# Attention block on one Trainium2 core: the low halves of the probabilities split by columns between VectorE and GpSimd

## Chip, cores, metric

One core of a Trainium2 chip. The metric is the device time of one execution in microseconds (us), the median of several runs. Lower is better.

## What is computed

For each of 16 images of 1024 tokens and 512 channels (all float32):

```
xn  = silu(group_norm(x, 32 groups) * scale + offset)
q, k, v = split(xn @ w_qkv)            # 8 heads of 64
P   = softmax(q k^T / 8)               # per head, 1024 x 1024
out = (P v) @ w_out + b_out + x
```

To keep float32-like accuracy with float16 matmuls, values are held as two float16 parts: a high part (the value rounded) and a low part (what the rounding lost). The probabilities have a high part `Ph` and a low part `Pl = P32 - Ph`, and both are multiplied with v.

## The kernel before

An image's attention is cut into 64 **units**. Unit v works on head v // 8, on one half (512) of the query tokens, and on two blocks of 128 keys; its exponentials are a tile of 128 rows by 1024 columns, in which columns 0 to 511 belong to the first key block (i = 0) and 512 to 1023 to the second (i = 1). The image has 4 steps of 16 units; `Fori` runs over images. Every engine walks through the same list of iterations (s, u), with v = 16 s + u, in an order written out by hand, and they meet only at semaphores. I number iterations by v within the image.

In iteration v, **TensorE** (L1009 to L1023) does: the scores of unit v into the PSUM tile `ST[v % 2]` (L970, L971), once exp_done tells that unit v - 2 has been read; the score maxima of a later unit into `TP` (L905), once VectorE has drained `TP`; the product of the probabilities of unit v - 2 with v (`times_v`, L976 to L1007, the matmuls at L1004); then a **side** job where the table `SIDE` (L79) has one. These are projections to q and k ("qk"), to v ("v") or to the output ("out"), each 12 matmuls of 512 columns (L891), and short transposes of the attention output ("ot", L941) or of the input ("xt", L947). In iterations 2, 6, 10, ... a "shift" (L912) comes last.

**ScalarE** in iteration v rounds the side result of iteration v - 1 to its high part (for example L521, L537), then writes the exponentials of unit v twice: `P32[v % 2]` in float32 (L559) and `Ph[v % 4]` in float16 (L562), which raises exp_done. `P32` has two buffers, so L559 of unit v waits until the low part of unit v - 2 has been made.

**VectorE** in iteration v (L777 to L803) copies the shift of v - 1 (L711), makes the low part of the side result of v - 1 (L650, L655, L662, or L667 for "out"), takes the maxima out of `TP` (L707, and every fourth time the small L699), and **in odd iterations only** makes the whole low part of unit v - 1 (`low_probs`, L755, L760). After that, in every fourth iteration, it adds up the sums of four units (L767, L768). At v = 7 it also moves half of v (L775, `move_v`). In iterations 28 to 31 it takes statistics of the next image's input (L721), in 38 it makes the coefficients of the group norm (L735 to L745), and from 40 to 47 eight pieces of the silu (L750, L753).

**GpSimd** in iteration v (L474 to L488) makes, **in even iterations only**, the whole low part of unit v - 1 (L460). In iterations 1, 5, 9, ... it normalises (L467), which waits for VectorE's sums of that same iteration. In iteration 37 it runs the Newton steps (L434 to L441), from 40 to 47 the low part of the silu pieces (L447), and now and then it adds the bias (L452).

So low parts of even units come from VectorE, which counts them in lo_dve, and those of odd units from GpSimd, which counts them in lo_pool. TensorE waits for one of the two before unit v's products (L981 to L984), ScalarE before L559 (L555 to L558). **SyncE** issues the DMAs, in order: the input (L330), the residual (L336), the output (L342), and after the last "qk" of a step six copies of q and k (`place`, L353).

Of the kernel before, what the change touches and what calls it, by code (L numbers as in the profile page):

```python
# [10 lines left out]
ALU = mybir.AluOpType  # L11
# [3 lines left out]
B, TOK, CH = 16, 1024, 512  # L15
# [5 lines left out]
HALF = 512  # L21
# [3 lines left out]
UNITS = 64  # L25
# [155 lines left out]
def wait(eng, sem, count):  # L181

    if not isinstance(count, int) or count > 0:
        eng.wait_ge(sem, count)


def conv_attention(nc, x, gamma, beta, w_qkv, w_out, b_out, out):
# [4 lines left out]
    with ctx:  # L192
# [109 lines left out]
        lo_dve = sem("lo_dve")  # L302
# [107 lines left out]
        def _(pool):  # L410
# [44 lines left out]
            def low_probs(b, v):  # L455

                pool.wait_ge(exp_done, UNITS * b + v + 1)

                wait(pool, pv_done, UNITS * b + v - 3)
                nc.gpsimd.tensor_tensor(Pl[:, v % 4, :], P32[:, v % 2, :], Ph[:, v % 4, :], ALU.subtract  # L460
                                        ).then_inc(lo_pool, 1)

            def normalise(b, half):
# [10 lines left out]
            def step(b, s, first=False, last=False):  # L474
                for u in range(16):
                    v = 16 * s + u
                    if v % 2 == 0 and not (first and v == 0):
                        low_probs(b, v - 1)
                    if v % 4 == 1 and not (first and v == 1):
                        normalise(b, v // 4 - 1)  # L480
                    if s == 2 and u == 5 and not last:
                        newton(b + 1)
                    if s == 2 and 8 <= u and not last:
                        low_xn(b + 1, u - 8)
                    if s == 3 and u < 4:
                        add_bias(b, u)
                    if (s, u) in LATE_BIAS and not first:
                        add_bias(b - 1, LATE_BIAS[s, u])  # L488
# [22 lines left out]
        def _(act):  # L511
# [40 lines left out]
            def exponentials(b, v):  # L552
                act.wait_ge(scores_ready, UNITS * b + v + 1)

                if v % 2 == 0:  # L555
                    wait(act, lo_dve, 32 * b + v // 2)
                else:
                    wait(act, lo_pool, 32 * b + v // 2)  # L558
                nc.scalar.activation(P32[:, v % 2, :], ST[:, v % 2, :], ACT.Exp, scale=cns[:, 0:1])  # L559

                wait(act, pv_done, UNITS * b + v - 3)
                nc.scalar.activation(Ph[:, v % 4, :], ST[:, v % 2, :], ACT.Exp, scale=cns[:, 0:1]  # L562
                                     ).then_inc(exp_done, 1)
# [51 lines left out]
        def _(dve):  # L615
# [139 lines left out]
            def low_probs(b, v):  # L755

                dve.wait_ge(exp_done, UNITS * b + v + 1)

                wait(dve, pv_done, UNITS * b + v - 3)
                nc.vector.tensor_tensor(Pl[:, v % 4, :], P32[:, v % 2, :], Ph[:, v % 4, :], ALU.subtract  # L760
                                        ).then_inc(lo_dve, 1)

            def sums(b, half):


                dve.wait_ge(pv_out, 16 * b + half + 1)
                nc.vector.reciprocal(den[:, half % 2, :], pv_sum[:, half % 2, :, HD])  # L767
                nc.vector.tensor_tensor(pv_sum[:, half % 2, 0:3, 0:HD], pv_sum[:, half % 2, 0:3, 0:HD],  # L768
                                        pv_sum[:, half % 2, 0:3, LO:LO + HD], ALU.add).then_inc(den_ready, 1)
# [7 lines left out]
            def step(b, s, cnt, first=False, last=False):  # L777
                for u in range(16):
                    v = 16 * s + u
                    for use in shift_before(s, u, last):  # L780
                        top_use(use, cnt)
                    for use in side_before(s, u, first, last):
                        side(use, image_before(use, b, s, u), cnt)
                    for use in unit_max(s, u, last):
                        top_use(use, cnt)
                    if v % 2 == 1:
                        low_probs(b, v - 1)
                    if v % 4 == 1 and not (first and v == 1):
                        sums(b, v // 4 - 1)
                    if s == 0 and u == 7:  # L790
                        move_v(b, cnt)
                    if s == 1 and u >= 12 and not last:
                        channel_stats(b + 1, 2 * u - 24, cnt)
                        channel_stats(b + 1, 2 * u - 23, cnt)
                    if s == 2 and not last:
                        if u == 1:


                            aggregate(b + 1)
                        if u == 6:  # L800
                            coefficients(b + 1)
                        if u >= 8:
                            silu(b + 1, u - 8)  # L803
# [72 lines left out]
            step(B - 2, 3, now)  # L876
            for s in range(4):
                step(B - 1, s, now, last=True)
            sums(B - 1, 15)
            for use in EPILOGUE:  # L880
                side(use, B - 1, now)
# [3 lines left out]
        def _(pe):  # L885
# [90 lines left out]
            def times_v(b, v, i, cnt):  # L976

                head, kp = v // 8, v % 4
                if i == 0:
                    pe.wait_ge(exp_done, UNITS * b + v + 1)  # L980
                    if v % 2 == 0:  # L981
                        pe.wait_ge(lo_dve, 32 * b + v // 2 + 1)
                    else:
                        pe.wait_ge(lo_pool, 32 * b + v // 2 + 1)  # L984
                    if kp == 0:

                        wait(pe, pv_out, 16 * b + v // 4)
                    if v == 0:
                        pe.wait_ge(side_drained, cnt.mark["v"])
                    if v == 32:  # L990
                        pe.wait_ge(v_moved, b + 1)
                kb = 2 * kp + i
                for qb in range(4):
                    at, to = i * HALF + qb * P, qb * (LO + HD)
                    v_all = V[:, kb, v_slot(head), :]
                    probs_hi, probs_lo = Ph[:, v % 4, at:at + P], Pl[:, v % 4, at:at + P]

                    products = [(slice(to, to + LO + HD), probs_hi, v_all[:, 0:LO + HD])]
                    if qb == 3:
                        products = [(slice(to, to + LO), probs_hi, v_all[:, 0:LO]),  # L1000
                                    (slice(to, to + HD), probs_hi, v_all[:, LO:LO + HD])]
                    products.append((slice(to, to + LO), probs_lo, v_all[:, 0:LO]))
                    for n, (cols, stationary, moving) in enumerate(products):
                        ins = nc.tensor.matmul(PV[:, cols], stationary, moving, start=kb == qb == n == 0,  # L1004
                                               stop=kb == TB - 1, skip_group_check=True)
                if i == 1:
                    ins.then_inc(pv_done, 1)  # L1007
# [73 lines left out]
```

## Time and profile before

| | |
|---|---|
| runs | 4330.39 us median of 3 (4330.1 to 4330.94) |
| the profiled execution | 4330.27 us, of which its span is 4328.5 us |
| TensorE busy | 3827.5 us (88%) |
| VectorE, ScalarE, GpSimd busy | 3022.1, 2851.5, 1717.7 us (70%, 66%, 40%) |
| mean granted TensorE clock | 0.958 |

Read the busy shares as averages over iterations of two kinds: in those with 12 matmuls of side work TensorE takes about 4.6 us or more, in those with none or a short one 2.0 to 2.6 us. One image takes 262.8 us. In rows of the timeline the number in brackets is the idle time of that engine before the instruction, and behind the arrow is what ended it.

### The profile page before, as it was taken

The numbers are of one execution on the slowest core, as the hardware profiler recorded it, in microseconds if no ns is written. First come the engines' busy times: TensorE is split into PE (matmuls) and PEld (weight loads), VectorE is DVE, ScalarE is ACT, GpSimd is POOL, SyncE is SP. The second block draws the span as 40 slices with busy tenths as digits, with TensorE's granted clock in tenths as the row PEclk, the third lists the DMA queues.
The fourth block names the chain that finished last, engine by engine and source line by source line (L and its number), as shares of the span: only waits on it lengthen the run. The fifth ranks groups of instructions, "written<-read, shape, count | busy, mean of one in ns | idle before, by whom it ended". The sixth has DMA issues, their size and how long they took to land.

```text
span 4328.5 us, 90413 instructions
## 1 busy us (share of the span) xinstructions
PE 3827.5 (88%) x32844; PEld 2133.3 (49%) x32844; DVE 3022.1 (70%) x3936; ACT 2851.5 (66%) x3202; POOL 1717.7 (40%) x1226
## 2 busy tenths in 40 slices
PE   3889999898998989989899998989989899898997
PEld 1445545454554545545455454545545455454553
DVE  5676676867767676676766768677676766767664
ACT  2676676767767676676766767667676766766664
POOL 1243443433434343343434434334343333434333
PEclk8989999999999999999999999999999999999999
DMA  2111112122021121212111121220311212121111
GB/s 75 37 38 47 57 30 74 31 59 60 16 82 36 50 55 32 73 30 59 45 47 57 30 74 31 59 59 16 82 37 50 55 31 74 30 59 45 40 54 36
DMA packets 105031, 211.25 MB, mean 49 GB/s; under 512 B 13392, under 2 KB 13392, under 8 KB 104656
## 3 DMA queue, kind: packets, MB, share of 16 engines
q1 hardware_dynamic: 104656, 205.84, 17.8%
q8 instruction: 286, 4.69, 0.5%
q14 instruction: 89, 0.73, 0.1%
HBM read 71.57 MB, written 33.55 MB: 24 GB/s over the span
## 4 chain that ended last, share of the span: by engine, by line
PE 52%; DVE 19%; issue 16%; ACT 4%; POOL 4%; SPq 2%; DMA 2%; DVEq 1%; POOLq 0%; ACTq 0%
PE SD L891 27%; PE PV L1004 9%; DVE Pl L760 5%; DVE mx L707 5%; PE TP L905 5%; PE ST L971 4%; PE ST L970 4%; POOL Pl L460 3%; SPq L353 2%; DVE work L750 2%; ACT QK L521 2%; DMA work<-in_x 1%; PE TP L912 1%; ACT Ph L562 1%; PE SD L947 1%
## 5 line engine op out<-in xcount | busy, mean ns | idle before, releaser
L559 ACT ACTIVATE P<-ST,cns 128x1024 f32<-128x1024 f32 x1024 | 1142.0, 1115 | 753.6 <-PE ST L971 536.3
L460 POOL TENSOR_TENSOR Pl<-P,Ph 128x1024 f16<-128x1024 f32 x512 | 1212.0, 2367 | 920.4 <-ACT Ph L562 917.3
L707 DVE TENSOR_REDUCE mx<-TP 128x1 f32<-128x1024 f32 x1024 | 1248.3, 1219 | 234.0 <-PE TP L905 223.8
L562 ACT ACTIVATE Ph<-ST,cns 128x1024 f16<-128x1024 f32 x1024 | 1134.8, 1108 | 0.0
L1004 PE MATMUL PV<-V,Ph 128*128 128x129 f16 (+2 forms) x10240 | 893.7, 213 | 133.9 <-DVE Pl L760 122.8
L1004 PEld LDWEIGHTS PV<-V,Ph 128*128 128x128 f16 x10240 | 790.6, 99 | 385.0 <-DVE Pl L760 150.7
L1004 PE MATMUL PV<-V,Pl 128*128 128x65 f16 x8192 | 861.9, 195 | 0.0
L970 PE MATMUL ST<-QK 128*128 128x512 f16 x2048 | 807.3, 394 | 0.4
L971 PE MATMUL ST<-QK 128*128 128x512 f16 x2048 | 807.1, 394 | 0.0
L1004 PEld LDWEIGHTS PV<-V,Pl 128*128 128x128 f16 x8192 | 740.1, 100 | 89.7 <-issue 17.1
L905 PE MATMUL TP<-QK 128*128 128x512 f16 x2048 | 640.6, 396 | 105.4 <-DVE QK L711 53.8
L891 PE MATMUL SD<-xn,wq 128*128 128x512 f16 x3072 | 707.1, 380 | 21.8 <-POOL xn L447 16.0
L467 POOL TENSOR_TENSOR O<-pv_sum,den 128x256 f32<-128x256 f32 x256 | 169.2, 661 | 1342.0 <-DVE pv_sum L768 1342.0
L760 DVE TENSOR_TENSOR Pl<-P,Ph 128x1024 f16<-128x1024 f32 x512 | 644.6, 1259 | 9.5 <-ACT Ph L562 9.5
L650 DVE SCALAR_TENSOR_TENSOR QK<-SD,sc,QK 128x512 f16<-128x512 f32 x256 | 191.7, 749 | 369.4 <-ACT QK L521 333.0
L891 PEld LDWEIGHTS SD<-xn,wq 128*128 128x128 f16 x3072 | 282.8, 98 | 329.4 <-issue 18.8
L521 ACT ACTIVATE QK<-SD,sc 128x512 f16<-128x512 f32 x256 | 175.9, 687 | 399.9 <-PE SD L891 399.9
L711 DVE CAST QK<-TP 64x512 f16<-64x512 f32 x256 | 175.9, 687 | 342.5 <-PE TP L912 342.1
L891 PE MATMUL SD<-wo,OT 128*128 128x512 f16 x1536 | 355.6, 381 | 51.2 <-DVE OT L662 45.3
L905 PEld LDWEIGHTS TP<-QK 128*128 128x128 f16 x2048 | 177.4, 100 | 430.0 <-DVE QK L711 165.4
L891 PE MATMUL SD<-wq,xn 128*128 128x512 f16 x1536 | 354.2, 380 | 10.2 <-DVE V L655 8.1
L970 PEld LDWEIGHTS ST<-QK 128*128 128x128 f16 x2048 | 207.4, 101 | 171.3 <-issue 18.0
(91 smaller groups left out, 2889.6 us busy)
## 6 DMA issues: line engine op xcount, KB each, us to landing
QK<-QK SPq DMA_DIRECT2D x384, 256.0 KB, 4.8
work<-in_x SPq DMA_DIRECT2D x128, 256.0 KB, 2.8
res<-in_x SPq DMA_DIRECT2D x128, 256.0 KB, 2.8
out<-res SPq DMA_DIRECT2D x128, 256.0 KB, 2.0
V<-in_L_conv_w_qkv SPq DMA_DIRECT2D x1, 3072.0 KB, 10.4
P<-in_L_conv_w_out SPq DMA_DIRECT2D x1, 1024.0 KB, 12.3
bias<-in_L_conv_b_out SPq DMA_DIRECT2D x1, 256.0 KB, 7.4
gam<-in_L_conv_gn_scale SPq DMA_DIRECT2D x1, 2.0 KB, 12.0
```

The costliest lines, as they stand in the source:

```text
L460: nc.gpsimd.tensor_tensor(Pl[:, v % 4, :], P32[:, v % 2, :], Ph[:, v % 4, :], ALU.subtract).then_inc(lo_pool, 1)
L521: nc.scalar.activation(QK[:, hi, bass.ts(half, HALF)], SD[:], ACT.Identity, scale=sc[:, col:col + 1]).then_inc(side_hi, 1)
L559: nc.scalar.activation(P32[:, v % 2, :], ST[:, v % 2, :], ACT.Exp, scale=cns[:, 0:1])
L562: nc.scalar.activation(Ph[:, v % 4, :], ST[:, v % 2, :], ACT.Exp, scale=cns[:, 0:1]).then_inc(exp_done, 1)
L650: nc.vector.scalar_tensor_tensor(out=QK[:, lo, cols], in0=SD[:], scalar=sc[:, col:col + 1], in1=QK[:, hi, cols], op0=ALU.mult, op1=ALU.sub ...
L707: nc.vector.reduce_max(mx[:, hh, qb:qb + 1], TP[:], AX.X).then_inc(top_drained, 1)
L760: nc.vector.tensor_tensor(Pl[:, v % 4, :], P32[:, v % 2, :], Ph[:, v % 4, :], ALU.subtract).then_inc(lo_dve, 1)
L891: ins = nc.tensor.matmul(SD[:], stationary(i, c), moving(j, c), start=(c == 0 and i + j == 0), stop=(c == CC - 1 and i == 1))
L905: ins = nc.tensor.matmul(TP[:, bass.ts(kh, HALF)], QK1[:, slot, 0, bass.ts(qb, P)], QK1[:, slot, 1, bass.ts(kh, HALF)], start=True, stop=True)
L970: nc.tensor.matmul(dst, QK1[:, slot, 1, kb], QK1[:, slot, 0, bass.ts(q, HALF)], start=True, stop=False)
L971: ins = nc.tensor.matmul(dst, QK2[:, slot, 1, kb], QK2[:, slot, 0, bass.ts(q, HALF)], start=False, stop=True)
L1004: ins = nc.tensor.matmul(PV[:, cols], stationary, moving, start=kb == qb == n == 0, stop=kb == TB - 1, skip_group_check=True)
```

## The change

For every unit VectorE makes the low part of columns 0 to 511 and GpSimd that of columns 512 to 1023. Both engines now call `low_probs(b, v - 1)` in every iteration. lo_dve and lo_pool each count every unit. ScalarE waits for both before L559. TensorE waits for lo_dve before the products of the first key block and for lo_pool before those of the second. A last `low_probs` on VectorE is added at the end, for the last unit.

```diff
@@ -457,7 +457,7 @@
                 pool.wait_ge(exp_done, UNITS * b + v + 1)
 
                 wait(pool, pv_done, UNITS * b + v - 3)
-                nc.gpsimd.tensor_tensor(Pl[:, v % 4, :], P32[:, v % 2, :], Ph[:, v % 4, :], ALU.subtract
+                nc.gpsimd.tensor_tensor(Pl[:, v % 4, HALF:], P32[:, v % 2, HALF:], Ph[:, v % 4, HALF:], ALU.subtract
                                         ).then_inc(lo_pool, 1)
 
             def normalise(b, half):
@@ -474,7 +474,7 @@
             def step(b, s, first=False, last=False):
                 for u in range(16):
                     v = 16 * s + u
-                    if v % 2 == 0 and not (first and v == 0):
+                    if not (first and v == 0):
                         low_probs(b, v - 1)
                     if v % 4 == 1 and not (first and v == 1):
                         normalise(b, v // 4 - 1)
@@ -552,10 +552,8 @@
             def exponentials(b, v):
                 act.wait_ge(scores_ready, UNITS * b + v + 1)
 
-                if v % 2 == 0:
-                    wait(act, lo_dve, 32 * b + v // 2)
-                else:
-                    wait(act, lo_pool, 32 * b + v // 2)
+                wait(act, lo_dve, UNITS * b + v - 1)
+                wait(act, lo_pool, UNITS * b + v - 1)
                 nc.scalar.activation(P32[:, v % 2, :], ST[:, v % 2, :], ACT.Exp, scale=cns[:, 0:1])
 
                 wait(act, pv_done, UNITS * b + v - 3)
@@ -757,8 +755,8 @@
                 dve.wait_ge(exp_done, UNITS * b + v + 1)
 
                 wait(dve, pv_done, UNITS * b + v - 3)
-                nc.vector.tensor_tensor(Pl[:, v % 4, :], P32[:, v % 2, :], Ph[:, v % 4, :], ALU.subtract
-                                        ).then_inc(lo_dve, 1)
+                nc.vector.tensor_tensor(Pl[:, v % 4, 0:HALF], P32[:, v % 2, 0:HALF], Ph[:, v % 4, 0:HALF],
+                                        ALU.subtract).then_inc(lo_dve, 1)
 
             def sums(b, half):
 
@@ -783,7 +781,7 @@
                         side(use, image_before(use, b, s, u), cnt)
                     for use in unit_max(s, u, last):
                         top_use(use, cnt)
-                    if v % 2 == 1:
+                    if not (first and v == 0):
                         low_probs(b, v - 1)
                     if v % 4 == 1 and not (first and v == 1):
                         sums(b, v // 4 - 1)
@@ -876,6 +874,7 @@
             step(B - 2, 3, now)
             for s in range(4):
                 step(B - 1, s, now, last=True)
+            low_probs(B - 1, UNITS - 1)
             sums(B - 1, 15)
             for use in EPILOGUE:
                 side(use, B - 1, now)
@@ -978,10 +977,6 @@
                 head, kp = v // 8, v % 4
                 if i == 0:
                     pe.wait_ge(exp_done, UNITS * b + v + 1)
-                    if v % 2 == 0:
-                        pe.wait_ge(lo_dve, 32 * b + v // 2 + 1)
-                    else:
-                        pe.wait_ge(lo_pool, 32 * b + v // 2 + 1)
                     if kp == 0:
 
                         wait(pe, pv_out, 16 * b + v // 4)
@@ -989,6 +984,7 @@
                         pe.wait_ge(side_drained, cnt.mark["v"])
                     if v == 32:
                         pe.wait_ge(v_moved, b + 1)
+                pe.wait_ge(lo_pool if i else lo_dve, UNITS * b + v + 1)
                 kb = 2 * kp + i
                 for qb in range(4):
                     at, to = i * HALF + qb * P, qb * (LO + HD)
```

## Rows read from the trace of the kernel before

**Rows 1.** The page, busy time of each engine

```profile
PE 3827.5 (88%) x32844; PEld 2133.3 (49%) x32844; DVE 3022.1 (70%) x3936; ACT 2851.5 (66%) x3202; POOL 1717.7 (40%) x1226
```

**Rows 2.** Groups by line and shape: busy us, mean ns | idle before, releasers

```profile
L460 POOL TENSOR_TENSOR Pl<-P,Ph 128x1024 f16<-128x1024 f32 x512 | 1212.0, 2367 | 920.4 <-ACT Ph L562 917.3 <-POOL gn L441 3.1
...
L760 DVE TENSOR_TENSOR Pl<-P,Ph 128x1024 f16<-128x1024 f32 x512 | 644.6, 1259 | 9.5 <-ACT Ph L562 9.5
...
L447 POOL TENSOR_TENSOR xn<-work,xn 128x512 f16<-128x512 f32 x128 | 150.1, 1173 | 246.6 <-DVE xn L753 246.6
...
L662 DVE TENSOR_TENSOR OT<-SD,OT 128x512 f16<-128x512 f32 x128 | 87.5, 683 | 17.1 <-ACT OT L537 14.1 <-DVE mv L727 3.0
...
L775 DVE COPY V<-V 128x4160 f16<-128x4160 f16 x16 | 50.7, 3170 | 0.0
...
L737 DVE TENSOR_TENSOR gn<-gn 128x4 f32<-128x4 f32 x16 | 32.0, 1998 | 0.5
```

**Rows 3.** Waits: us in total, times, the longest

```profile
ACT P L559 <- DVE Pl L760: 174.4, 306, 3.4
...
PE PV L1004 <- DVE Pl L760: 122.8, 217, 1.2
```

**Rows 4.** Timeline of TensorE, one image (1952.9 to 2215.7 us)

```profile
1952.91 0.38 PE L970 MATMUL ST<-QK 128*128 128x512 f16 x1
...
1954.82 0.23 PE L1004 MATMUL PV<-V,Ph 128*128 128x129 f16 x1 [0.45 <-DVE Pl L760]
...
1958.12 0.38 PE L970 MATMUL ST<-QK 128*128 128x512 f16 x1
...
1962.93 0.22 PE L1004 MATMUL PV<-V,Ph 128*128 128x129 f16 x1 [0.82 <-DVE Pl L760]
...
1973.82 0.38 PE L970 MATMUL ST<-QK 128*128 128x512 f16 x1
...
1978.41 0.38 PE L970 MATMUL ST<-QK 128*128 128x512 f16 x1
...
2085.07 0.23 PE L1004 MATMUL PV<-V,Ph 128*128 128x129 f16 x1 [0.25 <-DVE Pl L760]
...
2200.91 0.23 PE L1004 MATMUL PV<-V,Ph 128*128 128x129 f16 x1 [0.45 <-DVE Pl L760]
```

**Rows 5.** Timeline of VectorE and GpSimd, iterations 1 to 3 of that image

```profile
1959.35 0.75 DVE L650 SCALAR_TENSOR_TENSOR QK<-SD,sc,QK 128x512 f16<-128x512 f32 x1 [3.45 <-ACT QK L521]
...
1961.46 1.23 DVE L760 TENSOR_TENSOR Pl<-P,Ph 128x1024 f16<-128x1024 f32 x1
...
1969.23 1.22 DVE L760 TENSOR_TENSOR Pl<-P,Ph 128x1024 f16<-128x1024 f32 x1
...
1969.76 2.68 POOL L460 TENSOR_TENSOR Pl<-P,Ph 128x1024 f16<-128x1024 f32 x1 [3.96 <-ACT Ph L562]
```

**Rows 6.** Timeline, iterations 6 to 8: VectorE, then GpSimd, then TensorE

```profile
1981.77 0.68 DVE L711 CAST QK<-TP 64x512 f16<-64x512 f32 x1 [0.56 <-PE TP L912]
...
1984.30 1.22 DVE L760 TENSOR_TENSOR Pl<-P,Ph 128x1024 f16<-128x1024 f32 x1
1985.43 3.17 DVE L775 COPY V<-V 128x4160 f16<-128x4160 f16 x1
...
1984.83 2.66 POOL L460 TENSOR_TENSOR Pl<-P,Ph 128x1024 f16<-128x1024 f32 x1 [3.31 <-ACT Ph L562]
...
1989.34 2.75 PE L891 MATMUL SD<-wo,OT 128*128 128x512 f16 x12 [2.89 <-DVE OT L662]
```

**Rows 7.** Timeline of TensorE, iterations 39 and 47

```profile
2114.88 0.60 PE L905 MATMUL TP<-QK 128*128 128x512 f16 x2 [1.83 <-DVE QK L711]
...
2151.87 0.39 PE L905 MATMUL TP<-QK 128*128 128x512 f16 x1 [0.55 <-DVE QK L711]
```

**Rows 8.** Timeline of TensorE, from the products into the next iteration's scores

```profile
2001.79 0.19 PE L1004 MATMUL PV<-V,Pl 128*128 128x65 f16 x1
...
2001.82 0.38 PE L970 MATMUL ST<-QK 128*128 128x512 f16 x1
```

## The prediction, made before the changed kernel was run

> **What bounds the kernel now.** I started with the busy shares: TensorE is busy for 88% of the span, and GpSimd, the least busy, for 40% [rows 1]. So the change cannot win by freeing GpSimd. What it can touch is the 12% in which TensorE stands. The groups by line show that the low part on VectorE (L760) is hardly ever waiting for its input (9.5 us in all), so it starts late, while the one on GpSimd (L460) mostly starts as soon as the exponentials are there, 917 us of waiting for ScalarE [rows 2]. The waits say what this costs: TensorE stood 122.8 us in 217 places for VectorE's low part, and ScalarE was held by it 306 times [rows 3].
>
> The timeline of TensorE shows where. In one image, from 1952.91 us for 262.8 us, thirteen such stalls of 0.25 to 0.82 us stand, the first at 1954.82 and the last at 2200.91, 7.2 us together; the 217 are these thirteen in 16 images and a few more [rows 4]. All concern an even unit. A stall costs more than its idle time: two iterations with the same side work (a "qk") took 5.21 us (1952.91 to 1958.12, with a stall of 0.45) and 4.59 us (1973.82 to 1978.41, with none), 0.62 for 0.45, so 0.17 us on top [rows 4].
>
> The chain behind a stall: TensorE ends the side job of iteration 0, ScalarE makes its high part, VectorE the low part (L650 at 1959.35, after 3.45 us idle), then the maxima, then the whole low part of unit 0 from 1961.46 to 1962.69, and TensorE goes on at 1962.93 [rows 4, 5]. TensorE's own work in that time is short, since iteration 1 has only a transpose. ScalarE's wait for `P32` lies beside this and is not counted again.
>
> **The change, part by part.** All terms are for the profiled execution (4330.27 us; the median of the runs, 4330.39, is 0.1 us from it).
>
> 1. *VectorE's low part of even units is halved.* The whole takes 1.22 us [rows 5]; an operation on 128x512 of the same output takes 0.68 (L662) [rows 2]. It reads PSUM on one side, which this one does not, but 1.22 less a small fixed part, halved, gives the same. So it ends 0.54 us earlier. Of the thirteen places, twelve are worth at least 0.54 (0.43 idle and 0.17 on top are more), the smallest 0.25 + 0.17 = 0.42: 12 x 0.54 + 0.42 = 6.9 us an image, 217/13 x 6.9 = **-115 us**.
>
> 2. *VectorE gets a half low part for odd units*, 512 more instructions. 512 x 1.26 becomes 1024 x 0.68: 697 us for 645, so 52 us more busy [rows 2]. Where does it go? In iterations with a long side job it stands after the maxima, where VectorE then idles, 3.45 us before L650 [rows 5]. It is hidden there. If the cover were gone, 0.6 us would lie on the path in each of 512 units. It isn't covered in iterations 6 and 54, where only 0.56 us of idle lies ahead of the shift copy L711, which the next maxima wait for [rows 6]: I take 0.2 us for each, **+6 us**. In iterations 31 and 33 the new half is offset by the shorter one beside it, and the 0.54 of item 1 stands.
>
> 3. *GpSimd.* 512 x 2.37 becomes 1024 x about 1.17, the price of its 128x512 subtraction L447 [rows 2]. That is the same total. Its half is ready long before VectorE's, and the wait for it moves to the second key block. No stall.
>
> 4. *GpSimd's shorter instruction holds VectorE for less time.* This is not in the diff, but the rows show it. `move_v` was issued at 1985.43 and took 3.17 us, while the GpSimd low part that had asked at 1984.83 ran to 1987.49, having itself lasted 2.66 because VectorE's L760 was under way. All 16 copies take 3170 ns, and L737, four columns wide, took 2.0 us on average [rows 2, 6]. In such pairs one engine stands until the other has finished. By this the copy alone needs about 1.1 us. TensorE waits 2.89 us in iteration 8 for L662, which stands behind the copy [rows 6]. After the change L760 ends 0.54 earlier, and GpSimd, whose instruction is 1.17 long, holds VectorE for about 1.1 where it held it for 2.06 (1985.43 to 1987.49), so the copy ends 0.54 + 0.96 = 1.5 us earlier: 16 x 1.5 = **-24 us**. In iteration 38 the same holds L737, and TensorE stands 1.83 us in 39 [rows 7]; but now a second GpSimd half (unit 38's) is queued right behind the first and can hold L739, so of 1.5 us I keep 0.4: 15 x 0.4 = **-6 us**. Among the silu pieces the holds are in 42 and 46; I take 0.4 and 0.3, the latter about half of the 0.55 stall in 47 [rows 7]: 15 x 0.7 = **-10 us**. The bounds for these three are the whole stalls (2.9, 1.8 and about 1.7 us), and on the other side nothing, or 0.5 us lost in each of the eight silu iterations (60 us), because more but shorter instructions clash.
>
> 5. *Waits.* TensorE has one wait more per unit, between two key blocks, ScalarE one more before L559. A wait already satisfied costs TensorE nothing that shows: the scores, which wait for exp_done, start 0.03 us after the last product, the distance that these products keep anyway [rows 8]. I take nothing; the bound is 0.03 x 1024 = 31 us. Behind a wait for lo_pool stands only what waited for the whole low part before. SyncE's queue has no step moved.
>
> 6. *The end.* The last unit's low part is two halves at once where it was one on GpSimd: about -1 us.
>
> Sum: -115 + 6 - 24 - 6 - 10 - 1 = **-150 us**, so 4330 - 150 = **4180 us**.
>
> **A rule against this change.** In the rows above a VectorE and a GpSimd operation that both read SBUF did not overlap. The two halves of a unit become ready at the same exp_done. The Trainium skill ("SBUF — State Buffer", section "SBUF: two separate sides") says that an instruction of VectorE with two SBUF inputs and one of GpSimd that reads SBUF take a shared pair of ports as an exclusive lock, the later one blocked for the whole of the other. By that rule the trace agrees, with 3.17 us for the copy, and the gain of splitting a unit would be gone wherever the halves meet. Do they meet? VectorE's comes to unit n only after the maxima, GpSimd's at exp_done. Unit 2: VectorE starts at 1969.23, GpSimd's next (unit 3, at its exp_done) at 1969.76, 0.53 us later. Unit 2's own GpSimd half is over by then. In iterations 1, 5, 9, ... GpSimd stands at the normalising, which waits for VectorE's sums, so it is out of the way. Halved, VectorE's part ends at 1969.91, and GpSimd is delayed by 0.1, not VectorE [rows 5].
>
> **Rivals.**
>
> *Slower: GpSimd gets in first.* If VectorE reaches its half more than 0.53 us later than now in the critical iterations, or ends up behind GpSimd's halves there in general, it stands for 1.17 us and then works 0.68, 1.85 for 1.22 before: +0.63 x 217 = +137, less the 40 of item 4: **about 4427 us**. For it: the measured holds. Against it: the lead of 0.53, and nothing in item 2 that delays the critical chain. Chance 0.07.
>
> *Half of it: another wait follows close.* In one image TensorE also stands for maxima, shift copies and DMAs. If VectorE's new halves push the maxima back by 0.3 us in the critical iterations, or if the clashes in the silu iterations cost what item 4 gives, half of item 1 and item 4's first term stay: -57 - 24 = -81, and + 15 to 30 for clashes: **about 4270 us**. Chance 0.2.
>
> *No change: TensorE waits for the extra semaphores or GpSimd is late*, so that all is given back. It would need both bounds (31 and 60) and half the gain at once. Or the halves are made but the stalls move to L711 and L707 one for one: **4330 us**. Chance 0.04.
>
> *More than forecast*: the copy goes ahead of GpSimd (2.5 us in place of 1.5, 16 us) and the stalls of items 1 and 4 vanish entirely, 217 x 0.74 = 161 in place of 115: **about 4100 us**. Chance 0.06.
>
> **How the numbers follow.** The forecast (4130 to 4235) has 0.63. The likeliest is 4180. The range reaches down to 4130, a third of the way to what removing every such stall gives, and up to 4285, past the half case. Outside stay the slower and the unchanged case and most of the large gain, about 0.15. Within 0.2% (8.7 us, what a measurement of this kernel can tell) 0.04, slower 0.07, faster 0.89.
>
> **What would show it.** Right: L760 x1024 at about 0.68 us, with few over 1.2; L460 x1024 at 1.17 to 1.3; the wait of TensorE for L760 down from 122.8 to under 35 us; L775 near 2.2 us; the stall in iteration 8 near 1.4. Wrong: a mean of L760 over 0.9 us (halves meet), TensorE waits for L460 or for L711 that grow by what L760's lost, or iterations 6, 54 and 40 to 47 longer than before.

## The result, and the profile after

The changed kernel takes **4211.68 us** (median of 4 runs, 4207.9 to 4217.09) against 4330.25 for the kernel before in the same comparison: 0.9728 of it, 95% interval 0.9711 to 0.9745, 119 us less. 4180 was forecast, in a range of 4130 to 4285. The four runs lie in pairs, two near 4208 us at a mean granted clock of 0.963 and 0.965, two near 4216 at 0.959. The profiled execution is the 4207.9 one, with a span of 4206.0 us, 122.5 less than before.

The page and the groups by line of the changed kernel (the same statements stand in other lines there: L758 was L760 before, L1000 was L1004, L969 was L970, L557 was L559, L904 was L905, L709 was L711, L660 was L662, L684 was L686, and L733 to L743 were L735 to L745):

```profile
PE 3803.3 (90%) x32844; PEld 2130.5 (51%) x32844; DVE 3103.1 (74%) x4448; ACT 2846.6 (68%) x3202; POOL 1778.6 (42%) x1738
...
L460 POOL TENSOR_TENSOR Pl<-P,Ph 128x512 f16<-128x512 f32 x1024 | 1263.9, 1235 | 1198.1 <-ACT Ph L560 1186.6
...
L758 DVE TENSOR_TENSOR Pl<-P,Ph 128x512 f16<-128x512 f32 x1024 | 803.0, 784 | 6.3 <-ACT Ph L560 5.9
```

The waits:

```profile
PE TP L904 <- DVE QK L709: 70.8, 50, 2.6
...
ACT P L557 <- DVE Pl L758: 49.7, 77, 2.3
...
PE PV L1000 <- DVE Pl L758: 20.9, 71, 1.0
```

VectorE is busier by 81 us (52 were forecast: its half takes 0.784 us on average, not 0.68), and yet TensorE's wait for it is down from 122.8 us in 217 places to 20.9 in 71 [rows 3]. ScalarE's is down from 174.4 to 49.7. TensorE's wait for the shift copy has grown, from 53.8 to 70.8 us.

TensorE's timeline, iterations 0 to 2, the start of 3, and 8 of the same image as in [rows 4]; an iteration begins at its first L969:

```profile
1906.24 0.38 PE L969 MATMUL ST<-QK 128*128 128x512 f16 x1
...
1911.00 0.38 PE L969 MATMUL ST<-QK 128*128 128x512 f16 x1
...
1913.52 0.38 PE L969 MATMUL ST<-QK 128*128 128x512 f16 x1
...
1915.16 0.22 PE L1000 MATMUL PV<-V,Ph 128*128 128x129 f16 x1 [0.18 <-DVE Pl L758]
...
1918.84 0.38 PE L969 MATMUL ST<-QK 128*128 128x512 f16 x1
...
1940.03 2.75 PE L890 MATMUL SD<-wo,OT 128*128 128x512 f16 x12 [1.54 <-DVE OT L660]
```

Iteration 0 took 4.76 us (5.21 before). In iteration 2 a stall of 0.82 is left as 0.18, and the wait in iteration 8 fell from 2.89 to 1.54 [rows 4, 6].

From such starts I worked out each of the 64 iterations as a mean over images 1 to 14. An image went from 262.92 to 255.17 us, 7.75 us less:

| iterations | forecast, us an image | measured |
|---|---|---|
| the thirteen places (0, 2, 10, 12, 18, 22, 32, 34, 48, 50, 56, 58, 60) | -6.9 | -6.63 |
| 8 (the copy) | -1.5 | -1.51 |
| 39 (the coefficients) | -0.4 | **+2.02** |
| 40 to 47 (silu) | -0.7 | -1.47 |
| 6 and 54, the shift copy | +0.4 | 0.00 |
| 4, 20, 24, 28 | 0 | -0.62 |
| all others | 0 | +0.46 |

Among the others, iteration 35 got 0.46 us shorter, and this was not foreseen either. Before, it had no stall but a granted clock of 0.73 to 0.76 and took about 6.1 us; in the changed kernel TensorE waits 0.93 us there for the shift copy, the clock is 1.00 and the iteration takes 5.69 us (13 of the 14 images). So some 7 us of the gain came with the higher clock of this iteration; why it no longer falls there stays open.

One row of the table is badly wrong, iteration 39. What happened there shows in the timeline of VectorE, then GpSimd, then TensorE, of the changed kernel; TensorE began iteration 37 at 2049.93, 38 at 2054.80 and 39 at 2059.62:

```profile
2051.46 0.94 DVE L684 TENSOR_SCALAR gn<-gn 128x4 f32<-128x4 f32 x1
...
2054.02 0.69 DVE L758 TENSOR_TENSOR Pl<-P,Ph 128x512 f16<-128x512 f32 x1
...
2054.72 0.33 DVE L766 TENSOR_TENSOR pv_sum<-pv_sum 128x192 f32<-128x192 f32 x1
...
2057.52 0.68 DVE L758 TENSOR_TENSOR Pl<-P,Ph 128x512 f16<-128x512 f32 x1
...
2059.41 0.16 DVE L733 TENSOR_TENSOR gn<-gam,gn 128x4 f32<-128x4 f32 x1 [1.21 <-POOL gn L441]
2059.60 1.16 DVE L735 TENSOR_TENSOR gn<-gn 128x4 f32<-128x4 f32 x1
2060.80 1.08 DVE L737 TENSOR_TENSOR gn<-bet,gn 128x4 f32<-128x4 f32 x1
...
2062.46 0.68 DVE L709 CAST QK<-TP 64x512 f16<-64x512 f32 x1
...
2057.66 0.60 POOL L441 TENSOR_TENSOR gn<-gn,nt 128x4 f32<-128x4 f32 x1
...
2059.59 2.27 POOL L460 TENSOR_TENSOR Pl<-P,Ph 128x512 f16<-128x512 f32 x2 [0.22 <-POOL gn L441]
...
2063.19 1.04 PE L904 MATMUL TP<-QK 128*128 128x512 f16 x2 [2.54 <-DVE QK L709]
```

The same place in the kernel before, where TensorE began iteration 38 at 2107.21:

```profile
2111.05 0.16 DVE L735 TENSOR_TENSOR gn<-gam,gn 128x4 f32<-128x4 f32 x1 [1.03 <-POOL gn L441]
2111.24 2.13 DVE L737 TENSOR_TENSOR gn<-gn 128x4 f32<-128x4 f32 x1
```

In the changed kernel two GpSimd halves stand back to back (units 37 and 38), and each holds one four-column operation of VectorE, 1.16 and 1.08 us. Before there was one hold of 2.13, so nothing was saved on the holds themselves. The forecast had seen the second half coming, and still kept 0.4 of the copy's 1.5 us, a figure in which VectorE comes 0.54 us earlier. It came later: the first coefficient began 4.61 us into iteration 38, not 3.84. Ahead of it VectorE had an odd half more, and its four-column L684 was held for 0.94 us by GpSimd's half of unit 36, which is new there, so the sums and the Newton steps began 0.35 us later in iteration 38. One of the Newton steps (L441 at 2057.66) then took 0.60 us and not 0.20, beside VectorE's odd half of unit 37 (2057.52), which is new as well. The shift copy began 0.72 us later (2.84 us into iteration 39, before 2.12), so TensorE stood 2.54 us and not 1.83 [rows 7].

The other part is TensorE's clock. Stretches of iteration 39, in an image of each kind (columns: length, busy us of each engine, granted clock, DMA share, GB/s), changed kernel:

```profile
2059.62:2068.56 8.94, 6.39 (x39) 3.23 (x37) 5.88 (x10) 4.18 (x5) 3.40 (x3) 0.81 0.00 0
3337.98:3345.30 7.32, 4.77 (x40) 2.39 (x38) 5.89 (x10) 4.19 (x5) 3.41 (x3) 1.00 0.00 0
```

and the kernel before:

```profile
2112.03:2118.62 6.59, 4.76 (x39) 2.39 (x37) 6.45 (x10) 4.18 (x5) 3.46 (x2) 1.00 0.00 1
```

The same work kept TensorE busy for 6.39 us where the clock fell (0.81 in the mean, part of the stretch at 1.2 GHz in place of 2.4), and for 4.77 where it did not. It fell behind the stall in 11 of the 14 images. So, against the kernel before, iteration 39 has 0.73 us of longer stall (7.32 - 6.59) in every image, and 1.62 of lower clock (8.94 - 7.32) where it fell.

### The profile page after: what moved, and what is told of

The parts are those of the page before. It is cut to its first block, busy times and chain, and to the rows that moved or that the text cites. A ratio compares the mean times of both kernels' runs of the same rounds, so it can differ in the third digit from the quotient of the medians.

```text
span 4206.0 us, 93255 instructions
## 1 busy us (share of the span) xinstructions
PE 3803.3 (90%) x32844; PEld 2130.5 (51%) x32844; DVE 3103.1 (74%) x4448; ACT 2846.6 (68%) x3202; POOL 1778.6 (42%) x1738
## 4 chain that ended last, share of the span: by engine, by line
PE 63%; DVE 14%; issue 13%; ACT 3%; POOL 3%; SPq 2%; DMA 2%; DVEq 0%; POOLq 0%; ACTq 0%
PE SD L890 29%; PE PV L1000 12%; PE TP L904 7%; PE ST L970 6%; PE ST L969 6%; DVE mx L705 4%; DVE Pl L758 3%; SPq L353 2%; DMA work<-in_x 2%; PE SD L946 1%; PE TP L911 1%; POOL Pl L460 1%; ACT QK L521 1%; DVE QK L648 1%; DVE work L748 1%
## 5 line engine op out<-in xcount | busy, mean ns | idle before, releaser
L460 POOL TENSOR_TENSOR Pl<-P,Ph 128x512 f16<-128x512 f32 x1024 | 1263.9, 1235 | 1198.1 <-ACT Ph L560 1186.6
L557 ACT ACTIVATE P<-ST,cns 128x1024 f32<-128x1024 f32 x1024 | 1142.9, 1116 | 596.1 <-PE ST L970 503.0
L1000 PEld LDWEIGHTS PV<-V,Ph 128*128 128x128 f16 x10240 | 793.2, 99 | 268.7 <-ACT Ph L560 83.8
L1000 PE MATMUL PV<-V,Ph 128*128 128x129 f16 (+2 forms) x10240 | 890.7, 213 | 37.8 <-DVE Pl L758 20.9
L1000 PE MATMUL PV<-V,Pl 128*128 128x65 f16 x8192 | 862.5, 195 | 0.8 <-issue 0.8
L758 DVE TENSOR_TENSOR Pl<-P,Ph 128x512 f16<-128x512 f32 x1024 | 803.0, 784 | 6.3 <-ACT Ph L560 5.9
L969 PE MATMUL ST<-QK 128*128 128x512 f16 x2048 | 796.7, 389 | 0.1
L970 PE MATMUL ST<-QK 128*128 128x512 f16 x2048 | 796.5, 389 | 0.0
L1000 PEld LDWEIGHTS PV<-V,Pl 128*128 128x128 f16 x8192 | 738.2, 100 | 93.4 <-issue 14.4
L904 PE MATMUL TP<-QK 128*128 128x512 f16 x2048 | 634.6, 392 | 115.5 <-DVE QK L709 70.8
L904 PEld LDWEIGHTS TP<-QK 128*128 128x128 f16 x2048 | 174.2, 99 | 436.6 <-DVE QK L709 184.3
L709 DVE CAST QK<-TP 64x512 f16<-64x512 f32 x256 | 176.0, 687 | 175.5 <-PE TP L911 174.8
L969 PEld LDWEIGHTS ST<-QK 128*128 128x128 f16 x2048 | 205.4, 100 | 167.4 <-issue 11.9
```

Of the source, the lines that this page charges most:

```text
L460: nc.gpsimd.tensor_tensor(Pl[:, v % 4, HALF:], P32[:, v % 2, HALF:], Ph[:, v % 4, HALF:], ALU.subtract).then_inc(lo_pool, 1)
L758: nc.vector.tensor_tensor(Pl[:, v % 4, 0:HALF], P32[:, v % 2, 0:HALF], Ph[:, v % 4, 0:HALF], ALU.subtract).then_inc(lo_dve, 1)
L904: ins = nc.tensor.matmul(TP[:, bass.ts(kh, HALF)], QK1[:, slot, 0, bass.ts(qb, P)], QK1[:, slot, 1, bass.ts(kh, HALF)], start=True, stop=True)
L969: nc.tensor.matmul(dst, QK1[:, slot, 1, kb], QK1[:, slot, 0, bass.ts(q, HALF)], start=True, stop=False)
L970: ins = nc.tensor.matmul(dst, QK2[:, slot, 1, kb], QK2[:, slot, 0, bass.ts(q, HALF)], start=False, stop=True)
```

## Experiments

**1. The coefficients ahead of GpSimd's half** (coef_first)

```diff
 # GpSimd, step(), ahead of low_probs(b, v - 1)
+                    if s == 2 and u == 6 and not last:
+                        pool.wait_ge(coef_ready, b + 2)
```

> The changed kernel, in which GpSimd waits for the coefficients of the group norm (coef_ready) before it makes its half of unit 37. Theory A (the changed kernel's long iteration 39 comes from GpSimd halves that hold VectorE's small operations twice, 1.16 and 1.08 us, and from the lower TensorE clock behind the long stall): both small operations fall to 0.16 us, TensorE's wait in iteration 39 falls from 2.54 to about 0.5 us, the clock there stays at 1.0, iteration 39 goes from 8.6 to about 5.3 us, 15 x 3.3 = 50 us less, about 4160 us. Rival B (it is only that the sums, and with them the Newton steps, come later): the stall stays above 2 us and the time is within 15 us of the changed kernel's.

Measured: 4168.39 us (0.9626 of the kernel before, 0.9610 to 0.9642), 43 less than the changed kernel. Timeline of VectorE and TensorE there, and the stretch of iteration 39:

```profile
2036.19 0.16 DVE L735 TENSOR_TENSOR gn<-gam,gn 128x4 f32<-128x4 f32 x1 [1.20 <-POOL gn L441]
2036.38 0.16 DVE L737 TENSOR_TENSOR gn<-gn 128x4 f32<-128x4 f32 x1
2036.58 0.16 DVE L739 TENSOR_TENSOR gn<-bet,gn 128x4 f32<-128x4 f32 x1
...
2037.32 0.68 DVE L711 CAST QK<-TP 64x512 f16<-64x512 f32 x1
...
2038.05 0.60 PE L906 MATMUL TP<-QK 128*128 128x512 f16 x2 [0.62 <-DVE QK L711]
...
2036.40:2041.86 5.46, 4.83 (x40) 2.44 (x38) 3.97 (x10) 3.56 (x5) 2.97 (x3) 1.00 0.00 0
```

The operations fall to 0.16 us, the stall to 0.62, the clock stays at 1.00 and iteration 39 is 3.1 us shorter (8.60 to 5.45 in the mean). Theory A holds, and its numbers nearly (50 us were expected, 43 came); some 0.4 us an image came back elsewhere, where iteration 35 got 0.57 us longer at a lower clock (about 0.74, from 1.00).

**2. No odd halves on VectorE** (odd_whole_pool)

```diff
 # GpSimd, low_probs
+                lo = HALF if v % 2 == 0 else 0
-                ... Pl[:, v % 4, HALF:] ...
+                ... Pl[:, v % 4, lo:] ...
 # VectorE, step()
-                    if not (first and v == 0):
+                    if v % 2 == 1:
                         low_probs(b, v - 1)
```

with the waits of ScalarE and TensorE to match.

> The changed kernel, but split in even units only; the low parts of odd units are whole on GpSimd as before, so VectorE has no odd halves. Theory A (the gain is the shorter VectorE operation on the chain of even units, and GpSimd's shorter operation where it holds VectorE): the thirteen places gain as in the changed kernel, iteration 8 is back at its long stall (+0.96 us an image), iteration 39 changes by under 1 us, in all about 4225 us. Rival B (the odd halves on VectorE cost much, by work or clashes): removing them brings the time to 4150 us or less. Rival C (the gain came from halving odd units): back above 4300 us.

Measured: 4219.92 us (0.9745, 0.9728 to 0.9761), 8 more than the changed kernel, a difference that the two intervals do not quite separate. The thirteen places keep what they had gained, to 0.1 us, but for iteration 34 (+0.21). So halving odd units gains nothing there, and the odd halves on VectorE cost at most 0.08 us in each. Elsewhere they do cost: iterations 29, 33 and 37 went from 4.76, 3.00 and 4.86 us to 4.59, 2.65 and 4.63. Iteration 8 went from 6.29 to 8.91 us: its copy is held for 3.17 us again, and the clock falls. The first line is from the groups by line, the second the stretch of iteration 8:

```profile
L775 DVE COPY V<-V 128x4160 f16<-128x4160 f16 x16 | 50.7, 3170 | 0.0
...
1934.57:1943.45 8.88, 6.37 (x38) 2.89 (x36) 5.66 (x5) 3.22 (x4) 3.68 (x2) 0.81 0.49 116
```

That is more than the 0.96 us expected, because of the clock. Iteration 39 got 0.92 us shorter (7.68), with the clock at 1.0 in 13 of 14 images, although its stall is longer (2.80). The first coefficient begins 3.95 us into iteration 38 there, 0.66 us earlier than in the changed kernel, since the two odd halves ahead of it are gone; but the whole low part of unit 37 and the half of unit 38 then hold VectorE for 2.13 and 1.07 us.

**3. The low part first in VectorE's iteration**, of the changed kernel (low_first_split) and of the kernel before (low_first_whole)

```diff
 # VectorE, step()
+                    if not (first and v == 0):      # low_first_whole: if v % 2 == 1
+                        low_probs(b, v - 1)
                     for use in shift_before(s, u, last):
...
-                    if not (first and v == 0):
-                        low_probs(b, v - 1)
```

> The changed kernel with VectorE's half placed first in its iteration, ahead of the shift copy and the side result, where VectorE idles in most iterations. Theory A (position in the chain is what counts): TensorE's wait for the low part falls from 20.9 us to about 5, a mean iteration 2, 10, 50, 58 falls by 0.2 to 0.3 us; but VectorE now meets GpSimd's half of the same unit at exp_done, so the mean of its low part rises above 0.9 us and in short iterations the shift copy comes later: 4160 to 4220 us. Rival B (halves that become ready together cost as the lock rule says, on the path): slower than the changed kernel by over 40 us.

> The kernel before (whole units by turns), with VectorE's whole low part placed first in its iteration. Theory A (the 217 stalls come from where the low part stands in VectorE's order, behind the side result and the maxima, so taking it off the chain is worth as much as halving it): TensorE's wait for it falls from 122.8 to under 20 us and the time from 4330 to about 4200 us, in spite of the shift copy that comes later in iterations 7 and 55. Rival B (VectorE's amount of work bounds those stretches): the stalls reappear as waits for the maxima, 4300 us or more.

Measured: 4256.85 us (0.9829, 0.9813 to 0.9846) and 4289.17 us (0.9905, 0.9888 to 0.9921). Both missed. In the second, TensorE's wait for the low part is all but gone (0.2 us), which is theory A's first half, but look at what took its place. Waits of low_first_whole:

```profile
PE TP L905 <- DVE QK L711: 207.2, 203, 3.2
```

and its VectorE in iterations 6 and 7 (the copy of the shift stands behind a low part that itself waited):

```profile
1961.01 1.22 DVE L760 TENSOR_TENSOR Pl<-P,Ph 128x1024 f16<-128x1024 f32 x1 [0.49 <-ACT Ph L562]
1962.15 0.68 DVE L711 CAST QK<-TP 64x512 f16<-64x512 f32 x1
```

The wait for the shift copy rose from 53.8 to 207.2 us. I had expected this in iterations 7 and 55 only (+1.06 us each); it also came in 11, 19, 23, 27 and 31 (0.35 to 0.68 each), in 51 (+1.28), and in the silu iterations, among others. With halves the transposed outputs and the "out" results were late too: in low_first_split TensorE waited 0.65 us in iteration 2 and 1.00 in iteration 30. So VectorE's idle time ahead of the side result is no free room of 1.2 us: what takes it away is an exp_done that comes shortly before. Position and length of the low part both count, and shortening it is the cheaper of the two. VectorE's mean low part in low_first_split was 819 ns, 35 more than in the changed kernel, and not over 900 as expected. But the clash of both halves of a unit at exp_done was there: GpSimd's mean rose from 1235 to 1415 ns, and in iteration 30 the clash lies on the path. GpSimd, VectorE and TensorE there, in low_first_split:

```profile
2043.73 1.16 POOL L460 TENSOR_TENSOR Pl<-P,Ph 128x512 f16<-128x512 f32 x1
...
2044.19 1.25 DVE L758 TENSOR_TENSOR Pl<-P,Ph 128x512 f16<-128x512 f32 x1
2045.35 0.74 DVE L665 SCALAR_TENSOR_TENSOR res<-SD,cns,res 128x512 f32<-128x512 f32 x1
...
2046.15 2.76 PE L890 MATMUL SD<-wo,OT 128*128 128x512 f16 x12 [1.00 <-DVE res L665]
```

The half took 1.25 us where it takes 0.68 alone, and the "out" result that TensorE waits for stands behind it. With 45 us more than the changed kernel, low_first_split lies where rival B put it (over 40), in part by its mechanism; how much of the 45 is the clash and how much the order was not separated.

**4. The two holds, of the copy and of the coefficients, taken away**, in the kernel before (before_no_holds) and in the changed one (split_no_holds)

```diff
 # GpSimd, step(), ahead of low_probs(b, v - 1)
+                    if s == 2 and u == 6 and not last:
+                        pool.wait_ge(coef_ready, b + 2)
+                    if s == 0 and u == 8:
+                        pool.wait_ge(v_moved, b + 1)
```

> The kernel before (whole units by turns) with two waits added on GpSimd: its low part of unit 7 waits for VectorE's copy (v_moved), that of unit 37 for the coefficients. Theory A (GpSimd's 2.1 us instruction holds VectorE while it runs, and TensorE waits behind): the copy falls from 3.17 to about 1.15 us and iteration 8 by 2.0 us, L737 from 2.0 to 0.16 us and iteration 39 by 1.8 us: 16 x 2.0 + 15 x 1.8 = 59 us, about 4271 us. Rival B (those instructions are long for another reason): durations and time as in the kernel before.

> The changed kernel with the same two waits. Theory A: as with the wait for the coefficients alone (4168 us), and the copy falls from 2.2 to about 1.15 us, so that TensorE's wait in iteration 8 falls from 1.54 to about 0.5: 16 x 1.05 = 17 us, about 4151 us. Against the kernel before with both waits this gives what splitting alone is worth, about 120 us. Rival B (GpSimd's half of unit 7, made later, becomes what TensorE waits for): no gain over 4168 us.

Measured: 4276.25 us (0.9874, 0.9857 to 0.9890) and 4145.38 us (0.9574, 0.9558 to 0.9590). The copy, by line, in the changed kernel as it is, then in before_no_holds; in split_no_holds (L777) it takes 1236 ns too:

```profile
1936.49 0.68 DVE L758 TENSOR_TENSOR Pl<-P,Ph 128x512 f16<-128x512 f32 x1
1937.09 2.20 DVE L773 COPY V<-V 128x4160 f16<-128x4160 f16 x1
...
1937.02 1.16 POOL L460 TENSOR_TENSOR Pl<-P,Ph 128x512 f16<-128x512 f32 x1 [2.01 <-ACT Ph L560]
```

```profile
L779 DVE COPY V<-V 128x4160 f16<-128x4160 f16 x16 | 19.8, 1236 | 0.0
```

The same copy took 3170, 2200 and 1236 ns, by what GpSimd was doing: a whole low part, a half, or nothing. That is the hold, measured by taking it away. The kernel before gains 54 us by two waits on GpSimd alone (59 expected: in iteration 39 TensorE now waits 1.23 us for GpSimd's low part of unit 37, which starts late and is 2.1 us long, so 0.5 us was gained there, not 1.8; iterations 26 and 35 together got 0.9 us shorter, which was not expected). Between the two kernels without these two holds lie **131 us**: that is what splitting is worth when they are out of the way. Of the 8.6 us an image, 6.5 are in the thirteen places, 0.5 in iteration 8 and 0.6 in iteration 39. split_no_holds is the best version of this study, 66 us below the changed kernel.

**5. The even half early** (even_half_early: split_no_holds with this)

```diff
 # VectorE, step()
                         top_use(use, cnt)      # shift_before
+                    if v % 2 == 1:
+                        low_probs(b, v - 1)
                     for use in side_before(s, u, first, last):
...
-                    if not (first and v == 0):
+                    if v % 2 == 0 and not (first and v == 0):
                         low_probs(b, v - 1)
```

> The one before this, with VectorE's half of even units placed ahead of the side result, but behind the shift copy; the odd halves stay behind the maxima. Theory A (what made the all-first placement slow was the shift copy and the transposed outputs standing behind odd halves): the last waits for the low part, 20.9 us, go, and nothing new shows: 4135 to 4150 us. Rival B (VectorE now meets GpSimd's half of the same unit in short iterations, and the side result is late): 4160 us or more.

Measured: 4217.87 us (0.9740, 0.9725 to 0.9756), 72 more than split_no_holds. This is rival B's result. Its VectorE from iteration 47 on, then TensorE's wait in 48:

```profile
2099.86 0.86 DVE L762 TENSOR_TENSOR Pl<-P,Ph 128x512 f16<-128x512 f32 x1
2100.75 0.75 DVE L657 SCALAR_TENSOR_TENSOR V<-SD,sc,V 128x512 f16<-128x512 f32 x1
2101.42 1.21 DVE L709 TENSOR_REDUCE mx<-TP 128x1 f32<-128x1024 f32 x1
...
2104.74 2.29 DVE L762 TENSOR_TENSOR Pl<-P,Ph 128x512 f16<-128x512 f32 x2
...
2102.69 0.60 PE L910 MATMUL TP<-QK 128*128 128x512 f16 x2 [0.63 <-DVE mx L709]
```

The even half, held by GpSimd, pushes the side result and the maxima back, and TensorE waits for those (0.63 us here; its wait for the maxima rose from 3.0 to 34.9 us in all). An odd half and the next even half can now stand side by side, as the two that take 2.29 us. The mean of L762 is 910 ns. The waits for VectorE's low part fell from 20.4 to under 3 us, for nothing.

**6. Other divisions of the columns** (columns_256, columns_768, columns_256_no_holds)

```diff
-                ... Pl[:, v % 4, HALF:] ...       # GpSimd
+                ... Pl[:, v % 4, 256:] ...        # columns_768: 768:
-                ... Pl[:, v % 4, 0:HALF] ...      # VectorE
+                ... Pl[:, v % 4, 0:256] ...       # columns_768: 0:768
 # TensorE, times_v
-                pe.wait_ge(lo_pool if i else lo_dve, UNITS * b + v + 1)
+                if i == 0:
+                    pe.wait_ge(lo_dve, UNITS * b + v + 1)
+                    pe.wait_ge(lo_pool, UNITS * b + v + 1)
```

> The changed kernel with 256 columns on VectorE and 768 on GpSimd, TensorE waiting for both before a unit's first product. Theory A: VectorE's operation falls to about 0.42 us, which is worth at most the 20.9 us of waiting that is left and some 10 us behind it, but GpSimd's instruction grows to about 1.7 us and holds longer: copy +0.5 us x 16, coefficients +1 us x 15 and the lower clock behind it, silu pieces: 4215 to 4245 us. Rival B (VectorE's work is the bound everywhere): 4180 us or less.

> The changed kernel with 768 columns on VectorE and 256 on GpSimd, TensorE waiting for both before a unit's first product. Theory A (the length of VectorE's operation stands on the chain of the thirteen places): 0.27 us more in each, 13 x 0.27 x 16 = 56 us, less 0.55 us for each hold by GpSimd (the copy, twice at the coefficients, which may also spare the lower clock in iteration 39, up to 40 us together): 4225 to 4260 us, and iteration 0 at 5.0 us, between 4.76 at 512 columns and 5.21 at 1024. Rival B (the split itself, not the length, is what helps): iteration 0 stays at 4.76 and the time falls, under 4200 us.

> The changed kernel with both GpSimd waits (as split_no_holds, 4145 us) and 256 columns on VectorE, 768 on GpSimd. Theory A (with the holds taken away, the shorter VectorE operation can only help: about 1.5 us an image in iterations 0, 2, 12, 18, 48 to 60): 4115 to 4140 us. Rival B (the lower TensorE clock in iteration 35, seen in most images with 256 columns, stays and costs 2.3 us an image): 4150 to 4170 us.

Measured: 4211.93 us (0.9725, 0.9709 to 0.9741), 4236.91 us (0.9784, 0.9768 to 0.9801) and 4150.23 us (0.9587, 0.9571 to 0.9603).

| columns on VectorE | 1024, by turns | 768 | 512 | 256 |
|---|---|---|---|---|
| iteration 0, us | 5.21 | 4.98 | 4.76 | 4.59 |
| iteration 2 | 5.88 | 5.58 | 5.31 | 5.19 |
| the copy, ns | 3170 | 1717 | 2200 | 1236 |
| iteration 39, us | 6.58 | 6.34 | 8.60 | 10.02 |
| kernel, us | 4330 | 4237 | 4212 | 4212 |

The 1024 of the table is the kernel before, the 512 the changed kernel. The result for 768 columns is inside what was expected, the one for 256 is 3 us under its theory A, and its copy went the other way. In the two new divisions TensorE waits for both engines before a unit's first product, which the changed kernel does not, so they differ from it by that as well.

Iteration 0 falls by 0.22 us for each quarter until its stall is gone at 4.59, the length that [rows 4] show without one. That is the chain, with VectorE's length as its last link. Two things go against it. With 256 columns GpSimd's instruction is 1.68 us long on average and holds the coefficients twice (iteration 39), while the copy goes free, since it is issued before GpSimd asks:

```profile
L460 POOL TENSOR_TENSOR Pl<-P,Ph 128x768 f16<-128x768 f32 x1024 | 1718.4, 1683 | 938.3 <-ACT Ph L560 929.0 <-PE PV L1002 5.7 <-POOL gn L441 3.1
L758 DVE TENSOR_TENSOR Pl<-P,Ph 128x256 f16<-128x256 f32 x1024 | 607.1, 593 | 7.2 <-ACT Ph L560 7.0
...
L737 DVE TENSOR_TENSOR gn<-bet,gn 128x4 f32<-128x4 f32 x16 | 23.6, 1474 | 0.5
L773 DVE COPY V<-V 128x4160 f16<-128x4160 f16 x16 | 19.8, 1236 | 0.0
```

With the two holds away, 256 columns came out 5 us above 512 (the intervals of the two overlap) and not the 5 to 30 us below that theory A wanted, as rival B said. Two stretches of iteration 35 of columns_256_no_holds, of neighbouring images:

```profile
2002.15:2010.92 8.77, 7.57 (x39) 3.51 (x37) 5.13 (x8) 2.12 (x2) 2.80 (x2) 0.61 0.01 2
2254.99:2260.95 5.96, 4.76 (x39) 2.39 (x37) 5.47 (x8) 2.12 (x2) 2.79 (x2) 1.00 0.01 3
```

The same 39 matmuls, 8.77 or 5.96 us, by the clock. Iteration 35 was long in 8 of 14 images. In front of it stand stalls in iteration 34, for the mean and the shift, and one of 1.2 us in 35 itself. Against split_no_holds, 1.1 us an image is won up to iteration 33 and 1.1 from iteration 48 on; iteration 35 loses 1.8, and iteration 39 loses 0.9, where TensorE waits 0.8 us for GpSimd's longer part.

## Why the prediction was right, and where it was not

**Item 1, the shorter low part on the chain: right.** -6.63 us an image for -6.9, and the quarters of experiment 6 confirm its working, the 0.17 us on top of a visible stall too: iteration 0 still takes 4.76 us with no stall in its rows, and 4.59 with 256 columns. Overlooked were iterations 4, 20, 24 and 28, which show no stall in the rows either and were 0.15 us longer before.

**Item 2, the odd halves: right in kind.** They are hidden in the idle time of long iterations, to the 0.08 us of experiment 2. The 6 us for iterations 6 and 54 did not come. They do cost where VectorE was full already, around iterations 29 to 37: 29, 33 and 37 got longer by 0.10, 0.25 and 0.23 us, which I had taken as nothing; experiment 2, without odd halves, has all of this back. VectorE's half takes 784 ns on average, not 680, while its median is 683. I put the difference, 107 us over 1024 of them, down to holds by GpSimd, of which few fell on the chain; no run separates it.

**Items 3 and 5, GpSimd's half and the waits: right.** GpSimd's low parts take 52 us more than before (1263.9 for 1212.0), and TensorE's wait for it is 2.0 us in all. Iterations without a stall have the same length as before to 0.01 us (4.59, 2.00, 2.09), so 1024 more waits on TensorE cost nothing.

**Item 4, the holds.** The copy was right: 1.51 us for 1.5, and experiment 4 takes the hold away and gets the 1.24 us that was worked out as 1.1. **The coefficients were the term that failed**: "of 1.5 us I keep 0.4" came out as +2.02, a miss of 2.4 us an image, some 36 us, which is more than the 32 between forecast and result. The other misses come to about 1 us an image the other way. The second hold had been foreseen. The 1.5 us were taken over from the copy, with 0.54 us of VectorE coming earlier in them. Missed were that VectorE reaches this place 0.77 us later, by an odd half, a new hold on L684 and a held Newton step, and that the longer stall is followed by a stretch at the lower clock. Nothing in the forecast had a price for the clock. It also worked the other way in iteration 35 (0.46 us an image gained), so a part of the agreement between 4180 and 4212, some 7 us, is luck. The silu iterations gained twice what was taken, 0.4 us each in 43 and 44 and 0.6 in 47; why was not looked into.

**The rule that speaks against the change.** Both halves of a unit do become ready at once, and holds are everywhere in this trace. The argument that VectorE comes 0.53 us ahead in the critical iterations held: none of the thirteen lost. The Trainium skill ("SBUF — State Buffer", section "SBUF: two separate sides") counts among the instructions that take the shared ports those of one input in a two-port mode; the trace agrees, with L684 at 0.94 us for 0.17 and the copy at 3.17, 2.20 and 1.24, though no row tells the mode. Here the price of the holds was paid off the critical path, but for the copy and iteration 39; where VectorE's half was moved to exp_done it fell on the path (iteration 30 of low_first_split).

**The rivals.** "Slower" did not happen, nor "no change". "Half of it" named the shift copies: their wait did rise, 53.8 to 70.8 us: by 13 us in iteration 35 and 11 in iteration 39, against 7 less in iteration 47. The maxima, which that rival named too, were not pushed back: TensorE's wait for them (L904) fell from 7.4 to 4.0 us. The large gain of the last rival (4100) needed the stalls gone entirely, and 4145 is what the removal of two holds reached. The range's lower end, 4130, lies 50 of the 80 us on the way from 4180 to that 4100, and not a third of it as the forecast says.

What stays open is why the clock falls behind the stall of iteration 39 in 11 images and not in 3, two of which have the same stall (2.55 us, the third 2.46). Between those two images and the 11 nothing else differs in the rows that I read.

## What to carry to other kernels

Splitting one operation between two engines pays when it is the last link of a chain that a third engine waits for, even though the total work grows (here by 81 us on VectorE and 61 on GpSimd). Read first where the operation stands, and ask what ended the waits, not how busy the engines are. Count with VectorE and GpSimd as with two users of one lock, and look in the trace for small operations with long durations; where such a one is on the path, let GpSimd wait for it; two such waits were worth 54 us together in the kernel before, with no other change. A new stall near a busy stretch can cost more than its length by the clock (1.62 us on top in iteration 39), so look at the granted clock of that stretch before pricing it.

## What was not expected of the hardware

- Behind a stall of 2.54 us the granted clock was 0.81 over iteration 39 (8.94 us for 7.32), while behind 2.89 us in iteration 8 of the kernel before it stayed at 1.0, and behind 2.51 us in iteration 8 of odd_whole_pool it was 0.81, in each of these two in all 14 images. In odd_whole_pool a stall of 2.84 us in iteration 39 left it at 1.0 in 12 of the 13 images that have it. Iteration 35 had 0.75 with no stall before and 1.00 behind a stall of 0.93 us after. The length of one stall does not decide it alone.
- An operation of four columns on VectorE took 0.16 us or 1.16 us, and one with a single tensor input (L684) took 0.94 us, by what GpSimd was running. GpSimd is held in turn: a Newton step in coef_first took 0.60 us in place of 0.20 behind VectorE's half.
